# The first normalised rows of a cross attention, prepared two rounds earlier

## The chip, the cores and the metric

The kernel runs on one core of one Trainium2 chip, as one program. Its engines work side by side, each through its own instructions in a fixed order: TensorE (PE) multiplies matrices and transposes, ScalarE (ACT), VectorE (DVE) and GpSimd (POOL) work on elements, and SyncE (SP) issues transfers. Semaphores are the only ties between them. The metric is device time of one execution in microseconds (us), the median of several runs.

## The reference

Four transformer layers follow one another on `x` of 8 batches x 128 rows x 256 numbers, in float32, each attending to the same context. What matters here is where the second ends and the third begins:

```
def _gqa_forward(hidden_state, encoder_hidden_state, ...):      # second layer, 32 heads of 8
    ...
    out = out @ Wo + bo
    x = out + hidden_state
    return (x - mu) * rsqrt(var + EPS) * gamma + beta

def _forward(x, xf_1, xf_2, ...):                               # third layer
    h = _layer_norm(x, ln1_scale, ln1_offset)
    x = res + _cross_attention(h, xf_1, wq1, bq1, wk1, bk1, ...)  # 16 heads of 128
    ...
# in _cross_attention: qh = q_in @ wq + bq ; kh, vh from the context
```

The queries of the third layer need the rows of `x` after the second layer's output, its normalisation and a second one. Keys and values need the context alone.

## The kernel before

`x` lies in on-chip memory (SBUF) as eight batches of 128 rows. The second layer's small heads (`SmallHeads`) run in 16 rounds `r`, two per batch. They are pipelined in an order written out by hand: step `t` of the loop holds the scores of round `t` and later stages of earlier rounds, and steps `R` to `R + 5` (`R` = 16) only empty the pipeline. In step `R + 4` the last batch is transposed (L1167, evacuated by ACT at L1249), multiplied by the output weights (`output(7)`, L1173) and added to `x` by DVE (`add_x(7)`, L1314).

This tail already holds work of the next layer. `n1` is the second layer's normalisation over rows (`statistics` with L1363 and `finish` with L1375, POOL computes the reciprocal deviation at L781 and L783), `first` = `cross.norms[0]` the first normalisation of the third. Batches go in pairs `c`; pairs 0 and 1 are treated in the tail, pairs 2 and 3 later. In steps `R + 2` to `R + 5` PE also projects the cross attention's first four groups of keys (`pe_key`, L1590), which ACT evacuates (`act_key`, L1711).

The third and fourth attention (`CrossLayers`) then start with a part ahead of their loop: PE projects the values of units 0 and 1 (`project_v`, L1618), each followed by the 4 transposes of one pair of normalised rows (`Norm.transposes`, L822); ACT evacuates them with scale and offset into `hT` (L831) and copies them rounded into the high half of `split_sources` (L839); POOL forms the low half, the remainder (`low`, L846). A matmul of this layer is six matmuls, three products of high and low halves for each of two chunks. Then two groups of queries (L1590 again, evacuated by ACT at L1715) need the low halves of batches 0 to 3 (`norm.lo` 4) and the evacuated third and fourth key.

The loop has 128 units of two heads; in step `t` stand the scores of unit `t` (L1632), the transposes of unit `t - 1` (L1643), a projection, the values of unit `t + 2`, the context of unit `t - 2`, the output of unit `t - 3`. DVE takes the maxima (L1808), normalises the probabilities (L1816) and evacuates values (L1803); in its steps 0 to 4 it also handles pairs 2 and 3, beginning with `finish` in step 0. POOL's queue ahead of the loop holds the first value bias (L1882) and small copies of learnt keys (L1904), `low` of pairs 0 and 1, the reciprocal deviations of pairs 2 and 3, `low_wo(0)` (L1897), `low_v(1)` (L1891) and a second value bias.

Of the kernel before, what the change touches and what calls it, by code (L numbers as in the profile page):

```python
# [149 lines left out]
def wait(e, count, value):  # L150

    if isinstance(count, Count):
        e.wait_ge(count.sem, count.base + value)
    else:
        e.wait_ge(count, value)
# [858 lines left out]
class SmallHeads:  # L1014
# [88 lines left out]
    def pe(self, e):  # L1103
        g, l0, project = self.g, self.l0, self.project
# [32 lines left out]
        def context(r):  # L1137
            b, m = self.unit(r)
            if r == 0:
                wait(e, project.vs, 1)  # L1140
            wait(e, self.pt0, r + 1)
            wait(e, self.pt1, r + 1)
            if r >= 1:
                wait(e, self.ot, r)
            PT = self.PT[r % 2]
            for c in range(4):
                mm = e.matmul(self.bC[32 * c:32 * c + 32, :], self.vx[:, b, 4 * m + c, :],
                              PT[:, 512 * c:512 * c + 512], start=True, stop=True)
            mm.then_inc(self.c_full.sem, 1)

        def claim(after):
            if self.last_use:
                wait(e, *self.last_use)
            self.last_use = after
# [35 lines left out]
        for t in range(self.R + 6):  # L1190
            if 0 <= t - 4 < self.R:
                back_transposes(t - 4)
            if t < self.R:
                scores(t)
            if t == 0:
                l0.sum_transposes(e, 6)
                l0.sum_transposes(e, 7)
            if t in (1, 2, 7):
                n = {1: 4, 2: 5, 7: 6}[t]
                claim((project.qk, n + 1))  # L1200
                project.pe_group(e, n)
            if 0 <= t - 2 < self.R:
                transposes(t - 2, 0)
            if self.last_of_batch(t - 5):
                normalised_transposes(self.unit(t - 5)[0])
            if 0 <= t - 3 < self.R:
                context(t - 3)
            if self.last_of_batch(t - 5):
                output(self.unit(t - 5)[0])
            if t == 8:  # L1210
                claim((project.qk, 8))
                project.pe_group(e, 7)
            if t in (9, 11, 13, 15):
                rows_of_first_layer(4 + (t - 9) // 2)
            if 0 <= t - 2 < self.R:
                transposes(t - 2, 1)
            if self.cross and t >= self.R + 2:
                self.cross.pe_key(e, t - self.R - 2)


    def act(self, e):
        g = self.g

        def exps(r, half):
            s = self.sm[r % 3]
            whole = slice(1024 * half, 1024 * half + 1024)
            wait(e, self.shifted, 4 * r + 2 * half + 2)
            a = e.activation(s[:, whole], s[:, whole], ACT.Exp)
            a.then_inc(self.exp.sem, 1)

        def evacuate_t(r, half):
            wait(e, self.t_full, 2 * r + half + 1)
            if r >= 2:
                wait(e, self.c_full, r - 1)
            e.activation(self.PT[r % 2][:, 1024 * half:1024 * half + 1024],
                         self.bT[:, :, :].rearrange("p n t -> p (n t)"), ACT.Copy)\
                .then_inc((self.pt0, self.pt1)[half].sem, 1)

        def evacuate_c(r):
            wait(e, self.c_full, r + 1)  # L1240
            if r >= 2:
                wait(e, self.tb_full, r - 1)
            e.activation(self.oT[r % 2], self.bC[:, :], ACT.Copy).then_inc(self.ot.sem, 1)

        def evacuate_ct(b):
            wait(e, self.ct_full, b + 1)
            if b >= 2:
                wait(e, self.o_full, b - 1)
            e.activation(self.cxT[:, b % 2, :], self.bX[:, 0:D], ACT.Copy).then_inc(self.cx.sem, 1)  # L1249

        for b in range(4, B):
            self.l0.raw(e, b)
        for t in range(self.R + 6):
            if 0 <= t - 2 < self.R:
                exps(t - 2, 1)
            if self.last_of_batch(t - 5):
                evacuate_ct(self.unit(t - 5)[0])
            if 0 <= t - 2 < self.R:
                evacuate_t(t - 2, 0)
            if 0 <= t - 3 < self.R:  # L1260
                evacuate_c(t - 3)
            if t in (1, 2, 7):
                self.project.act_group(e, {1: 4, 2: 5, 7: 6}[t])
            if 0 <= t - 1 < self.R:
                exps(t - 1, 0)
            if t == 8:
                self.project.act_group(e, 7)
            if t in (9, 11, 13, 15):
                self.l0.evacuate_x(e, 4 + (t - 9) // 2)
            if 0 <= t - 2 < self.R:  # L1270
                evacuate_t(t - 2, 1)
            if 3 <= t < 7:
                self.l0.scaled_h(e, t + 1)
            if self.cross and t >= self.R + 2:
                self.cross.act_key(e, t - self.R - 2)


    def dve(self, e):
        g, hd = self.g, self.hd
# [36 lines left out]
        for t in range(self.R + 6):  # L1316
            if 0 <= t - 4 < self.R:
                normalise(t - 4)
            if t < self.R:
                scale_and_mask(t)  # L1320
            if self.last_of_batch(t - 5):
                add_x(self.unit(t - 5)[0])
            if t < self.R:
                maxes(t)
            if t < 2:
                self.l0.stats(e, 4 + 2 * t)
                self.l0.stats(e, 5 + 2 * t)
            if t == 3:
                self.l0.shifts_of_h(e)
            if self.cross:  # L1330
                first = self.cross.norms[0]
                for c in range(2):
                    if t == self.R:
                        self.n1.statistics(e, c)
                    if t == self.R + 1 + c:
                        self.n1.finish(e, c)
                        first.statistics(e, c)
                    if t == self.R + 3 + c:
                        first.normalise(e, c)

    def drained(self):
# [78 lines left out]
class CrossLayers:  # L1420
# [174 lines left out]
    def pe_key(self, e, n):  # L1595
# [3 lines left out]
            wait(e, self.a1.pt1, self.a1.R)  # L1599
        self.project(e, self.first_keys[n])  # L1600

    def pe(self, e):
        g = self.g
        issued = {"t": 0, "v": 0}
# [70 lines left out]
        first = self.norms[0]  # L1675
        for c in range(2):
            project_v(c)
            first.transposes(e, c, g.acc[c])
        for m in self.first_queries:
            self.project(e, m)  # L1680
        for t in range(self.STEPS):
# [63 lines left out]
    def act(self, e):  # L1745
        g = self.g
# [14 lines left out]
                         ACT.Copy).then_inc(self.pt, 1)  # L1761

        first = self.norms[0]
        for c in range(2):
            first.evacuate(e, c, g.acc[c])
        e.wait_ge(self.q_bias, 1)
        self.high_wo(e, 0)
        for m in self.first_queries:
# [1011 lines left out]
```

## Time and profile before

| | before |
|---|---|
| runs, us (median of 3) | 1295.75 (1295.26 to 1298.41) |
| profiled execution, its own time | 1297.17 us |
| its span | 1295.4 us |
| PE busy | 1236.8 us (95%) |
| DVE, ACT, POOL busy | 813.8, 752.7, 569.6 us |
| chain of waits by engine | PE 82%, POOL 6%, DVE 5%, ACT 4% |
| mean granted clock of PE | 0.993 |

A row of the timeline is: start in us from the beginning of the span, duration in us, engine, line of the kernel, operation, what is written and read, count, and in brackets how long the engine had been idle before and what ended that. Several instructions of one kind in a row are merged into one. The chain of waits is followed back from the last instruction: each row has a start, a length and what the time went to; "issue" is time for which the profile shows no cause. A row of the windows has the stretch, its length, busy time with the number of instructions of PE, of PE's weight loads, of DVE, ACT and POOL, then the granted clock of PE as a share of the full one, the share of the transfer engines and GB/s. `l_cols`, `l_w` and the like are names from which a number was left out; `pS`, `pT`, `acc`, `heads_...` are banks of PSUM, where matmuls write.

### The profile page before, as it was taken

The page shows a single profiled execution, that of the slowest core. Times are in us where ns is not written, and L with a number is a line of the kernel's source. Part 1 is how long each engine was busy: PE and PEld are TensorE (multiplying, and loading weights), DVE is VectorE, ACT ScalarE, POOL GpSimd, SP SyncE. Part 2 cuts the span into 40 slices and gives each one's busy share as a digit, 9 for nine tenths or more (in the row PEclk, how much of TensorE's full clock was granted, in tenths as well). Part 3 has the DMA queues.
Part 4 walks back from the last instruction along what each step waited for, and adds up shares of the span by engine and source line. Part 5 has one row for each costly group of instructions (what it writes and reads, how often), then busy time and mean ns, then how long its engine had stood idle before and what let it go on. Part 6 is the DMA issues. An engine that isn't in the chain of part 4 may idle for free.

```text
span 1295.4 us, 24563 instructions
## 1 busy us (share of the span) xinstructions
PE 1236.8 (95%) x8928; PEld 1018.4 (79%) x8928; DVE 813.8 (63%) x1826; ACT 752.7 (58%) x2034; POOL 569.6 (44%) x601
## 2 busy tenths in 40 slices
PE   6999999999988997999999999999999898999899
PEld 5777777777754565899999988999999675878787
DVE  4666666866559785666666776666667514789610
ACT  4765666566557784654555565555554433888842
POOL 3665554556369784150212132322110314899710
PEclk9999999999999998999999999999999999999999
DMA  7101110010100004020202020202000100100000
GB/s 271 52 28 38 43 50 32 28 54 28 59 15 1 1 2 151 13 74 9 74 10 73 10 74 9 74 10 74 10 17 2 68 1 1 66 2 2 2 9 25
DMA packets 15525, 50.44 MB, mean 39 GB/s; under 512 B 1840, under 2 KB 5296, under 8 KB 14384
## 3 DMA queue, kind: packets, MB, share of 16 engines
q1 hardware_dynamic: 15408, 48.87, 11.1%
q8 instruction: 74, 1.21, 0.4%
q14 instruction: 43, 0.35, 0.1%
HBM read 47.82 MB, written 1.05 MB: 38 GB/s over the span
## 4 chain that ended last, share of the span: by engine, by line
PE 82%; POOL 6%; DVE 5%; ACT 4%; issue 2%; DMA 1%; SPq 0%; DVEq 0%; POOLq 0%; ACTq 0%
PE pS L1590 13%; PE pT L1618 7%; PE acc L1670 6%; PE acc L326 6%; PE pT L393 5%; PE pC L406 5%; PE pS L376 4%; PE pS L1632 4%; PE pC L1655 4%; PE acc L362 3%; PE heads_scores L1399 3%; PE heads_scores L1410 3%; POOL probs L2493 2%; PE pT L1643 2%; PE acc L418 2%
## 5 line engine op out<-in xcount | busy, mean ns | idle before, releaser
L1590 PE MATMUL pS<-split_sources,split_pair_weights 128*128 128x512 f32 x768 | 213.1, 413 | 5.8 <-issue 4.3
L717 POOL TENSOR_TENSOR probs<-probs,stats 128x512 f32<-128x512 f32 x128 | 130.5, 1040 | 140.3 <-DVE stats L588 140.3
L523 ACT ACTIVATE probs<-pS,stats 128x256 f32<-128x256 f32 x256 | 117.8, 472 | 99.4 <-DVE stats L583 99.4
L1760 ACT ACTIVATE probsT<-pT 128x256 f32<-128x256 f32 x128 | 49.2, 384 | 197.1 <-PE pT L1643 197.1
L1590 PEld LDWEIGHTS pS<-split_sources,split_pair_weights 128*128 128x128 f32 x768 | 136.5, 191 | 30.9 <-issue 6.6
L1670 PE MATMUL acc<-l_wo_parts,l_ctx_parts 128*128 128x256 f32 x768 | 121.9, 295 | 1.0 <-DVE l_ctx_parts L1832 1.0
L1618 PEld LDWEIGHTS pT<-l_wv_parts,split_sources 128*128 128x128 f32 x756 | 106.9, 188 | 14.2 <-issue 2.2
L1886 POOL TENSOR_TENSOR split_pair_weights<-weights_a,split_pair_weights 128x1024 fp32r<-128x1024 f32 x16 | 38.0, 2381 | 174.1 <-ACT split_pair_weights L1731 174.1
L1618 PE MATMUL pT<-l_wv_parts,split_sources 128*128 128x256 f32 x756 | 110.6, 281 | 2.1 <-issue 2.1
L326 PE MATMUL acc<-split_sources,split_pair_weights 128*128 128x512 f32 x372 | 99.5, 402 | 1.1 <-POOL split_pair_weights L699 0.7
L1670 PEld LDWEIGHTS acc<-l_wo_parts,l_ctx_parts 128*128 128x128 f32 x768 | 99.4, 190 | 1.2 <-DVE l_ctx_parts L1832 1.2
L583 DVE TENSOR_REDUCE stats<-pS 128x2 f32<-128x512 f32 x128 | 82.4, 685 | 28.0 <-PE pS L376 27.8
L1753 ACT ACTIVATE probs<-pS,stats 128x129 f32<-128x129 f32 x256 | 91.3, 366 | 3.5 <-DVE stats L1808 3.3
L1814 DVE RECIPROCAL stats<-stats 128x2 f32<-128x2 f32 x128 | 21.2, 166 | 102.6 <-ACT probs L1753 102.4
L1803 DVE TENSOR_TENSOR v<-pT,probs 128x256 f32<-128x256 f32 x126 | 53.4, 424 | 50.9 <-PE pT L1618 50.8
L1832 DVE SCALAR_TENSOR_TENSOR l_ctx_parts<-pC,l_cols,l_ctx_parts 128x128 fp32r<-128x128 f32 x256 | 78.1, 347 | 4.5
L393 PE MATMUL pT<-consts,probs 128*128 128x128 f32 x512 | 80.5, 280 | 0.1
L1655 PE MATMUL pC<-probsT,v 128*128 128x128 f32 x512 | 77.9, 274 | 1.9 <-DVE l_ctx_parts L1832 1.9
L326 PEld LDWEIGHTS acc<-split_sources,split_pair_weights 128*128 128x128 f32 x372 | 65.5, 189 | 13.0 <-POOL split_pair_weights L699 0.9
L393 PEld LDWEIGHTS pT<-consts,probs 128*128 128x128 f32 x512 | 58.7, 141 | 16.2 <-DVE probsT L592 0.5
L1655 PEld LDWEIGHTS pC<-probsT,v 128*128 128x128 f32 x512 | 67.9, 190 | 2.6 <-ACT probsT L1760 1.7
L376 PEld LDWEIGHTS pS<-l_keys_parts,l_queries_parts 64*128 64x128 f32 x768 | 49.3, 185 | 25.7 <-issue 16.9
(264 smaller groups left out, 2903.5 us busy)
## 6 DMA issues: line engine op xcount, KB each, us to landing
weights_a<-in_l_w SPq DMA_DIRECT2D x16, 768.5 KB, 4.2
weights_a<-in_l_w SPq DMA_DIRECT2D x16, 768.0 KB, 6.0
value_bias_rows<-in_l_bv SPq DMA_DIRECT2D x16, 256.0 KB, 4.5
weights_b<-in_l_wo SPq DMA_DIRECT2D x16, 256.0 KB, 2.6
w_fc<-in_l_w SPq DMA_DIRECT2D x4, 1024.0 KB, 5.8
bias_rows<-in_rows SPq DMA_DIRECT2D x1, 1536.0 KB, 13.5
x_residual<-in_x_dbl SPq DMA_DIRECT2D x2, 512.0 KB, 7.1
masked_scores<-in_ctx_dbl SPq DMA_DIRECT2D x2, 512.0 KB, 8.0
```

The source lines that it names most:

```text
L326: mm = e.matmul(bank[:, :], self.ws[i % 2][kw][:, q, 2 * (m % 2) + c, :], self.zu[c][ks][:, bs, ls], start=j == 0, stop=j == len(PARTS) - 1)
L376: mm = e.matmul(self.S[h][:, it, :], self.q[i % 2][kq][rows, s, it * P:it * P + P], self.k[i % 2][kk][rows, s, :], start=j == 0, stop=j == ...
L393: mm = e.transpose(g.pT[:, (2 * h + it) * P:(2 * h + it + 1) * P], self.E[:, n % 4, h, it, jt * P:jt * P + P], g.ident)
L523: a = e.activation(self.E[:, n % 4, h, it, :], self.S[h][:, it, :], ACT.Exp, bias=self.st[:, 1, n % 4, h, it:it + 1], accum_out=self.st[:, ...
L583: e.tensor_reduce(self.st[:, 1, n % 4, h, :], self.S[h], AX.X, ALU.max, negate=True)\
L717: e.tensor_tensor(self.E[:, n % 4, h, :, :], self.E[:, n % 4, h, :, :], self.st[:, 3, n % 4, h, :].unsqueeze(2).broadcast_to([P, 2, D]), A ...
L1590: mm = e.matmul(bank[:, :], self.w_qk[i % 2][kw][:, 1 - which, c, h * P:h * P + P], g.split[:, which, ks, c, half * HALF:half * HALF + HAL ...
L1618: mm = e.matmul(self.value_bank(n)[:, 0:D], g.split[:, 0, ks, c, b * P:b * P + P], self.w_v[i % 2][kw][:, c, :], start=j == 0, stop=j == l ...
L1655: mm = e.matmul(g.pC[:, h * P:h * P + P], g.v[:, n % B, h * P:h * P + P], self.PT[:, n % 2, h, :], start=True, stop=True)
L1670: mm = e.matmul(g.acc[b // 2][:, (b % 2) * D:(b % 2) * D + D], self.cx[:, n % 2, kc, h, :], self.wo[i % 2][kw][:, h, :], start=first and h ...
L1753: a = e.activation(self.E[:, n % 4, h, :], self.bS[:, h * (P + 1):(h + 1) * (P + 1)], ACT.Exp, bias=self.st[:, 1, n % 4, h:h + 1], accum_o ...
L1832: a = e.scalar_tensor_tensor(out=lo[:, h, :], in0=src[:, h, :], scalar=bias[:, h:h + 1], in1=hi[:, h, :].bitcast(F32), op0=ALU.add, op1=AL ...
```

## The change

The transposes of the pairs 0 and 1 and their evacuation move from the part ahead of the cross attention's loop into step `R + 4` of the heads' loop. On PE they stand behind the transposes of the last batch and ahead of its `output`; on ACT behind the evacuation of the last batch's transposes and ahead of the third and fourth key. DVE normalises pair 1 in step `R + 3`, right behind pair 0, ahead of `add_x(7)`. The banks stay the same; `pe_rows` waits until the heads' last scores have left them. POOL's and SP's orders stay as they are.

```diff
--- before.py
+++ after.py
@@ -1205,6 +1205,9 @@
                 normalised_transposes(self.unit(t - 5)[0])
             if 0 <= t - 3 < self.R:
                 context(t - 3)
+            if self.cross and t == self.R + 4:
+                self.cross.pe_rows(e, 0)
+                self.cross.pe_rows(e, 1)
             if self.last_of_batch(t - 5):
                 output(self.unit(t - 5)[0])
             if t == 8:
@@ -1271,6 +1274,9 @@
                 evacuate_t(t - 2, 1)
             if 3 <= t < 7:
                 self.l0.scaled_h(e, t + 1)
+            if self.cross and t == self.R + 4:
+                for c in range(2):
+                    self.cross.norms[0].evacuate(e, c, g.acc[c])
             if self.cross and t >= self.R + 2:
                 self.cross.act_key(e, t - self.R - 2)
 
@@ -1335,7 +1341,7 @@
                     if t == self.R + 1 + c:
                         self.n1.finish(e, c)
                         first.statistics(e, c)
-                    if t == self.R + 3 + c:
+                    if t == self.R + 3:
                         first.normalise(e, c)
 
     def drained(self):
@@ -1599,6 +1605,10 @@
             wait(e, self.a1.pt1, self.a1.R)
         self.project(e, self.first_keys[n])
 
+    def pe_rows(self, e, c):
+        wait(e, self.a1.scaled, self.a1.R)
+        self.norms[0].transposes(e, c, self.g.acc[c])
+
     def pe(self, e):
         g = self.g
         issued = {"t": 0, "v": 0}
@@ -1675,7 +1685,6 @@
         first = self.norms[0]
         for c in range(2):
             project_v(c)
-            first.transposes(e, c, g.acc[c])
         for m in self.first_queries:
             self.project(e, m)
         for t in range(self.STEPS):
@@ -1761,8 +1770,6 @@
                          ACT.Copy).then_inc(self.pt, 1)
 
         first = self.norms[0]
-        for c in range(2):
-            first.evacuate(e, c, g.acc[c])
         e.wait_ge(self.q_bias, 1)
         self.high_wo(e, 0)
         for m in self.first_queries:
```

PE's order from the heads' last steps to the queries, before (L1167 and L1173 are the last batch's transposes and output, L1590 keys and at the end queries, L1618 values, L822 the transposes of the rows):

```order
L1590 MATMUL pS<-split_sources,split_pair_weights 128x512 x6
L1167 MATMUL heads_output<-consts,v 128x128 x2
L1173 MATMUL heads_output<-w_fc,additive_mask 128x256 x2
L1590 MATMUL pS<-split_sources,split_pair_weights 128x512 x12
L1618 MATMUL acc<-l_wv_parts,split_sources 128x256 x6
L822 MATMUL acc<-consts,normalised 128x128 x4
L1618 MATMUL acc<-l_wv_parts,split_sources 128x256 x6
L822 MATMUL acc<-consts,normalised 128x128 x4
L1590 MATMUL pS<-split_sources,split_pair_weights 128x512 x12
```

and in the changed kernel, where L1596 is the projection and L1628 the values:

```order
L1596 MATMUL pS<-split_sources,split_pair_weights 128x512 x6
L1167 MATMUL heads_output<-consts,v 128x128 x2
L822 MATMUL acc<-consts,normalised 128x128 x8
L1173 MATMUL heads_output<-w_fc,additive_mask 128x256 x2
L1596 MATMUL pS<-split_sources,split_pair_weights 128x512 x12
L1628 MATMUL acc<-l_wv_parts,split_sources 128x256 x12
L1596 MATMUL pS<-split_sources,split_pair_weights 128x512 x12
```

The 8 transposes left the places behind each group of values and stand ahead of the output. Keys, values and queries follow one another.

ACT's order at the same place, before (L1711 key evacuations, L1249 the last batch, L831 and L839 the rows, L1715 queries):

```order
L1711 ACTIVATE kT<-pS,l_cols 128x4x128 x2
L1249 ACTIVATE additive_mask<-heads_output 128x256
L1711 ACTIVATE probs<-pS,l_cols 128x4x128 x2
L831 ACTIVATE hT<-acc,bias_cols 128x128 x4
L839 ACTIVATE split_sources<-hT 128x2x128 x2
L831 ACTIVATE hT<-acc,bias_cols 128x128 x4
L839 ACTIVATE split_sources<-hT 128x2x128 x2
L1743 ACTIVATE l_wo_parts<-weights_b 128x512
L1715 ACTIVATE qT<-pS,l_scaled_query_bias 128x512 x2
```

and in the changed kernel (L1720, L1252 and L1724 are the same three lines, L1752 is L1743):

```order
L1720 ACTIVATE kT<-pS,l_cols 128x4x128 x2
L1252 ACTIVATE additive_mask<-heads_output 128x256
L831 ACTIVATE hT<-acc,bias_cols 128x128 x4
L839 ACTIVATE split_sources<-hT 128x2x128 x2
L831 ACTIVATE hT<-acc,bias_cols 128x128 x4
L839 ACTIVATE split_sources<-hT 128x2x128 x2
L1720 ACTIVATE probs<-pS,l_cols 128x4x128 x2
L1752 ACTIVATE l_wo_parts<-weights_b 128x512
L1724 ACTIVATE qT<-pS,l_scaled_query_bias 128x512 x2
```

The last two keys' evacuations stand behind the rows instead of ahead of them.

DVE, from the heads' last `normalise` (L1305) on, before:

```order
L1305 TENSOR_TENSOR v<-heads_output,stats 128x128
L815 TENSOR_SCALAR normalised<-x_residual,stats 128x256 x2
L1314 TENSOR_TENSOR x_residual<-heads_output,x_residual 128x256
L815 TENSOR_SCALAR normalised<-x_residual,stats 128x256 x2
L1803 TENSOR_TENSOR v<-acc,probs 128x256 x2
L771 BN_STATS stats<-x_residual 128x6 x2
```

and in the changed kernel (L1311, L1320 and L1810 are the same lines as L1305, L1314 and L1803):

```order
L1311 TENSOR_TENSOR v<-heads_output,stats 128x128
L815 TENSOR_SCALAR normalised<-x_residual,stats 128x256 x4
L1320 TENSOR_TENSOR x_residual<-heads_output,x_residual 128x256
L1810 TENSOR_TENSOR v<-acc,probs 128x256 x2
L771 BN_STATS stats<-x_residual 128x6 x2
```

Pair 1 moved ahead of the last addition to `x`.

## Rows read from the trace of the kernel before

**Rows 1.** Windows: stretch, its us, then busy time and clock by engine.

```profile
484.00:492.00 8.00, 6.24 (x50) 3.76 (x49) 6.27 (x23) 5.61 (x8) 4.12 (x7) 1.00 0.01 3
...
497.00:503.50 6.50, 6.22 (x36) 5.34 (x36) 1.82 (x5) 2.71 (x7) 0.47 (x4) 1.00 0.51 184
...
503.50:507.79 4.29, 0.00 (x1) 0.03 (x1) 4.29 (x12) 3.52 (x11) 3.02 (x5) 0.91 1.02 375
...
507.79:510.50 2.71, 2.71 (x7) 2.13 (x8) 0.58 (x2) 0.00 (x0) 2.46 (x5) 0.50 0.87 328
```

**Rows 2.** Chain of waits, the end of the heads to the first scores.

```profile
497.28 1.13 PE heads_output L1173 x4
...
498.41 2.80 PE pS L1590 x12
...
501.20 0.71 PE acc L1618 x6
...
501.92 0.44 PE acc L822 x4
...
503.50 4.29 issue
...
507.79 5.47 PE pS L1590 x12
...
514.03 0.71 PE pS L1632 x4
```

**Rows 3.** Timeline, the heads' last step, four engines.

```profile
495.54 0.73 DVE L815 TENSOR_SCALAR normalised<-x_residual,stats 128x256 f32<-128x256 f32 x2
...
495.55 0.76 POOL L783 TENSOR_TENSOR stats<-stats,eps 128x2 f32<-128x2 f32 x1
...
496.06 0.38 PE L1167 MATMUL heads_output<-consts,v 128*128 128x128 f32 x2
...
496.23 0.72 POOL L1882 TENSOR_TENSOR probs<-value_bias_rows 128x256 f32<-128x256 f32 x1
...
496.85 0.38 ACT L1249 ACTIVATE additive_mask<-heads_output 128x256 f32<-128x256 f32 x1
```

**Rows 4.** Timeline, ACT and POOL while the normalised rows are prepared.

```profile
501.24 0.69 ACT L1711 ACTIVATE probs<-pS,l_cols 128x512 f32<-128x512 f32 x1 [0.72 <-PE pS L1590]
...
502.39 1.50 ACT L831 ACTIVATE hT<-acc,bias_cols 128x128 f32<-128x128 f32 x4 [0.46 <-PE acc L822]
...
504.28 1.60 POOL L846 TENSOR_TENSOR split_sources<-hT,split_sources 128x256 fp32r<-128x256 f32 x2 [6.81 <-ACT split_sources L839]
...
505.75 0.75 ACT L839 ACTIVATE split_sources<-hT 128x256 fp32r<-128x256 f32 x2
...
506.28 1.41 POOL L846 TENSOR_TENSOR split_sources<-hT,split_sources 128x256 fp32r<-128x256 f32 x2 [0.40 <-ACT split_sources L839]
```

**Rows 5.** Timeline, DVE: statistics without and beside POOL's subtractions.

```profile
484.30 0.74 DVE L771 BATCH_NORM_STATS2 stats<-x_residual 128x6 f32<-128x256 f32 x2
...
485.96 0.75 DVE L771 BATCH_NORM_STATS2 stats<-x_residual 128x6 f32<-128x256 f32 x2
...
504.39 1.77 DVE L1363 SCALAR_TENSOR_TENSOR x_residual<-x_residual,stats,bias_rows 128x256 f32<-128x256 f32 x2
```

**Rows 6.** Timeline, POOL, DVE and PE around the loop's first step.

```profile
510.04 1.28 POOL L1897 TENSOR_TENSOR l_wo_parts<-weights_b,l_wo_parts 128x512 fp32r<-128x512 f32 x1
...
511.27 1.30 POOL L1891 TENSOR_TENSOR l_wv_parts<-weights_a,l_wv_parts 128x512 fp32r<-128x512 f32 x1
...
515.12 0.87 DVE L1375 SCALAR_TENSOR_TENSOR x_residual<-x_residual,stats,bias_rows 128x256 f32<-128x256 f32 x2
...
517.54 0.41 PE L1643 MATMUL pT<-consts,probs 128*128 128x128 f32 x2 [0.23 <-DVE v L1803]
```

**Rows 7.** Timeline, DVE beside POOL in a later step of the loop.

```profile
758.66 2.38 POOL L1886 TENSOR_TENSOR split_pair_weights<-weights_a,split_pair_weights 128x1024 fp32r<-128x1024 f32 x1
...
759.79 1.54 DVE L1816 TENSOR_TENSOR probs<-probs,stats 128x256 f32<-128x256 f32 x1
```

## The prediction

> **What bounds the kernel now.** I read the page's share of the engines first: TensorE (PE) is busy for 95% of the span and holds 82% of the chain of waits, so time is won only where PE waits, or where its clock is low. The clock row of the page has one dip near the middle. The windows around it [rows 1] show what it is: PE works without a break until 503.50, has nothing to do for 4.29 us, and then runs at a granted clock of 0.50 (1.2 of 2.4 GHz). From 484 to 492, where it was busy for 6.24 of 8 us in shorter pieces, the clock stayed at 1.00. The chain of waits names the same place [rows 2]: the last output of the heads, two keys, the values, then "issue 4.29", and two query projections that take 5.47 us for 12 matmuls, where two key projections of the same shape took 2.80.
>
> What PE waits for at 503.50 stands in the code: a query projection needs `norm.lo` 4, the low halves of the first four batches of normalised rows. The timeline of ACT and POOL gives the order [rows 4]. The transposes of the rows stand behind the last output, two keys and a value; only then can ACT evacuate and round them (502.39 to 506.50), and POOL's last subtraction ends at 507.69, 0.10 before PE goes on. Yet DVE has the first pair of rows at 496.27 [rows 3]. PE waits for a chain ACT, POOL that starts 5 us later than its data allow.
>
> **The change part by part.** No instruction is added or removed: PE still issues 8 transposes, ACT 8 scale-and-shift evacuations and 4 copies, DVE 4 normalisations. All move.
>
> 1. *DVE.* The second pair is normalised directly behind the first, ahead of the last `add_x`. It needs its reciprocal deviation from POOL, ready at 495.55 + 0.76 = 496.31, when DVE is free. Unhindered the pair would take 0.73, to 497.1. But POOL starts the value bias at 496.23, for 0.72 [rows 3]. Below I show DVE and POOL keeping each other out; so the pair starts at 496.95 and ends at 497.6.
>
> 2. *PE.* The first 4 transposes fall into PE's wait for ACT (from 496.06 + 0.38 to 497.28 [rows 2, 3]) and cost nothing. The second 4 (0.44 [rows 2], then between the value groups) start at about 497.1 to 497.6, so that the last output starts at 497.6 to 498.1 instead of 497.28. I take 498.1, by the POOL row: 0.8 lost. `add_x(7)` and the loads that wait for it come as much later, which nothing near waits for.
>
> 3. *ACT.* It is free at 497.23 [rows 3]. Evacuations and copies took 505.75 + 0.75 - 502.39 = 4.11 [rows 4], so they now end at 501.3. The second pair is in its bank long before ACT comes to it. Behind them are now queued the third and fourth key evacuation, 0.69 each [rows 4], done at 502.0 and 502.7; the fourth was done at 501.9 before. PE needs the third for the first query, the fourth for the second.
>
> 4. *POOL.* Its last subtraction ended 1.19 after ACT's last copy (507.69 and 506.50); now at 502.5.
>
> 5. *PE again.* From its start at 498.1 the output takes 1.13, the keys 2.80, two value groups 0.71 each [rows 2]: the queries can start at 503.45. Rows (502.5) and third key (502.0) are there, with 0.9 to spare, so the wait of 4.29 is gone. PE has then no idle stretch before the queries, so they run as the keys do, 2.80, and end at 506.25. From the end of the queries to the first scores it was 514.03 - 513.26 = 0.77, ACT's evacuation; so scores at 507.0 instead of 514.0. As a sum: 4.29 (wait) + 2.67 (clock) + 0.88 (transposes out of the path) - 0.8 (late output) = **7.0 us**.
>
> 6. *What is late next.* DVE must be done with two value evacuations and the statistics of the other four batches. These started 503.52; without POOL beside them one pair takes 485.96 - 484.30 = 1.66 [rows 5]. Now values end at 504.0, statistics at 507.3. `finish` began 1.09 after the scores (515.12 and 514.03 [rows 2, 6]), with the first maxima just ahead of it; so DVE is wanted at about 507.7 and in time by 0.4. But POOL is not as far as before. Its chain follows DVE's statistics: last aggregate at about 506.6, a microsecond of reciprocal deviations (its longer instruction took 0.76 [rows 3]), then `low_wo` 1.28, `low_v` 1.30 and a value bias of 0.72, from 507.7 to 511. Before they lay from 510.04 on [rows 6], in DVE's idle time ahead of the first scores at 514.03; now they fall on the first step of the loop, on `finish` (two instructions, 0.87), then `normalise`. PE's first transposes stand behind all three.
>
> What that costs has rows of its own. A `normalise` of the loop took 1.54 us and ended at 761.33, 0.29 after the POOL subtraction that ran since 758.66 [rows 7]. Two scalings of `statistics` took 1.77 beside two POOL subtractions that took 1.60 [rows 4, 5], where the two of `finish`, of the same form, took 0.87 [rows 6]. Strictly, with the engines taking turns: `finish` asks at 508.1, gets in at 509.0, its second half at 510.7, `normalise` at 511.9. The first transposes, 3.51 after the scores before (517.54 - 514.03 [rows 2, 6]), or 510.5, would start at 512.6: 2.1 lost. At 0.45 each, as in rows 5 and 6 ((1.77 - 0.87) / 2), it is 1.35; with luck nothing. I take 2.0, since POOL's pieces here are long as in rows 7. PE works in order and has no idle time there to make it up. Net: 7.0 - 2.0 = **5.0 us**.
>
> The Trainium skill, SBUF — State Buffer, "SBUF: two separate sides", says that VectorE and GpSimd share a port pair as an exclusive lock: an instruction with two SBUF inputs, or a VectorE one in a two-port mode, waits for the whole of the other's. The two ends in rows 7 agree; it speaks for the 2.1 over the 1.35. By it the gain is 4.9, by 0.45 each 5.65.
>
> After the first steps every wait is relative to the loop's own beat, weights are loaded many steps ahead, and PE is the bound; a shift is kept to the end.
>
> The profiled execution took 1297.17 us, 1.42 more than the median of the runs, 1295.75. It would take 1292.2; the runs' median I put at 1295.75 - 5.0 = **1290.8**.
>
> **The rivals.**
> - *A, no collision.* POOL and DVE miss each other or the overlap is cheap; the output is only 0.3 late. Gain 7.0 + 0.5 - 0 = 7.5: 1288.3, down to 1289.7 with half of it. For it: POOL's pieces follow the end of DVE's statistics, and if these end half a microsecond earlier `low_wo` is over before `finish` asks. Against: `low_v` then takes its place, and rows 7.
> - *B, the clock falls anyway.* The tail of the heads is thin in PE work, and could bring the low level later, at the queries: 2.67 comes back and more of the first step. Gain 5.0 - 2.67 = 2.3 or less: 1293.4. Against: it stayed at 1.00 through 484 to 492 in the same tail.
> - *C, slower.* The low clock comes and lasts into the loop. A step holds 6 wide matmuls (1.4 at full clock, 2.7 at half), 6 of half their width and transposes, some 2 us more per step. With the queries' 2.67 gone too, 2.3 is left, so from the second slow step on the kernel is slower than before; three give 1299.5. Against: in rows 1 it came only behind 4.29 us of nothing.
> - *D, the wait moves.* The change doesn't do what it says: the second pair of rows, behind POOL's bias and its small copies, holds the output back by 2 to 3 us instead of 0.8, and keys, values and scores with it. PE then has the old idle time in another place. Gain 2.5 to 3.5: 1292.3 to 1293.3. Against: POOL's copies are 128x8.
>
> **How the numbers follow.** Forecast 0.53 (1289.7 to 1291.9), A 0.22, B 0.08, C 0.04, D 0.13. The range from A's end to B's and D's is 1288.0 to 1293.2, and leaves out C and the outer parts, under 0.2. A measurement here can tell about 0.3%, 3.9 us, from no change: the line is 1291.9. Below it lie A and nearly all of the forecast, 0.74; between are B, D and the forecast's edge, 0.22; slower 0.04.
>
> **What would show it.** In the profile after: 8 transposes at 496.4 to 498.1, ahead of the last output; no idle stretch of PE over 1 us from there to the scores; granted clock 1.00 throughout 497 to 520; the 12 query matmuls in about 2.8; first scores near 507; DVE's `finish` drawn out beyond 1.5 us beside `low_wo` and `low_v`, and PE waiting for DVE about 2 us before the first transposes of the loop. Steps from the third on should repeat before, shifted by 5. Wrong would be: a query that still waits for POOL, a low clock, or first scores later than 509; and, for the size, `finish` at 0.87 would make it 7.

## The result and the profile after

The changed kernel takes 1293.55 us (median of 12 runs, 1290.98 to 1294.46); the kernel before took 1296.84 in the runs made beside them (12 runs, 1295.02 to 1300.62). The ratio is 0.9969, with a 95% interval of 0.9961 to 0.9977: faster by 4.0 us (3.0 to 5.1). The two medians lie only 3.3 us apart, because the 12 runs of before hold the three that were known ahead of the forecast; the nine others have a median of 1297.62, to which the ratio fits. Forecast were a gain of 5.0 and a time of 1290.8 within 1288.0 to 1293.2. The time itself lies 0.35 us above that range. The kernel before also lay higher this time than the 1295.75 from which the forecast started, and 1295.75 times the ratio is 1291.7; so the gain is the number to compare.

The windows of the changed kernel (columns as in [rows 1]):

```profile
484.00:492.00 8.00, 6.24 (x52) 4.03 (x50) 6.30 (x23) 6.10 (x8) 4.63 (x8) 1.00 0.01 3
497.00:503.50 6.50, 5.95 (x35) 5.10 (x36) 1.64 (x4) 6.38 (x17) 4.03 (x9) 1.00 0.32 101
503.50:508.00 4.50, 3.72 (x20) 2.83 (x20) 3.92 (x14) 1.52 (x3) 2.12 (x4) 1.00 1.00 420
508.00:512.00 4.00, 2.69 (x18) 2.22 (x16) 3.80 (x5) 1.50 (x5) 3.83 (x4) 1.00 0.96 338
```

Where before had 4.29 us without PE work and then half the clock, PE is busy for 3.72 of 4.50 us and the clock stays at 1.00. What is new is the last row: PE busy for 2.69 of 4.00 us.

The chain of waits over the same place, beside [rows 2]:

```profile
496.86 1.11 DVE normalised L815 x2
...
498.11 0.63 PE acc L822 x4
498.74 0.87 PE heads_output L1173 x4
499.61 2.79 PE pS L1596 x12
502.40 1.43 PE acc L1628 x12
503.83 2.82 PE pS L1596 x12
...
507.41 0.73 PE pS L1642 x4
...
508.51 2.75 DVE x_residual L1381 x2
...
512.60 0.41 PE pT L1653 x2
```

The queries follow the values without a gap and take 2.82 us for 12 matmuls, and scores begin at 507.41 instead of 514.03. This profile runs half a microsecond late from the start (the heads' last maxima begin at 478.94; before, at 478.41), so the gain up to the scores is 6.62 + 0.53 = 7.15. Then the chain goes through DVE for 2.75 us, and PE's first transposes stand at 512.60, 5.19 behind the scores, where it had been 3.51 [rows 2, 6]. Gain there: 517.54 - 512.60 + 0.53 = 5.47.

Why DVE is late is in the timeline of DVE and POOL:

```profile
496.06 1.90 DVE L815 TENSOR_SCALAR normalised<-x_residual,stats 128x256 f32<-128x256 f32 x4
...
496.75 0.73 POOL L1889 TENSOR_TENSOR probs<-value_bias_rows 128x256 f32<-128x256 f32 x1
...
498.58 1.03 PE L1173 MATMUL heads_output<-w_fc,additive_mask 128*128 128x256 f32 x4
...
508.24 1.29 POOL L1904 TENSOR_TENSOR l_wo_parts<-weights_b,l_wo_parts 128x512 fp32r<-128x512 f32 x1
508.51 2.75 DVE L1381 SCALAR_TENSOR_TENSOR x_residual<-x_residual,stats,bias_rows 128x256 f32<-128x256 f32 x2
...
509.49 1.48 POOL L1898 TENSOR_TENSOR l_wv_parts<-weights_a,l_wv_parts 128x512 fp32r<-128x512 f32 x1
...
510.93 0.90 POOL L1889 TENSOR_TENSOR probs<-value_bias_rows 128x256 f32<-128x256 f32 x1
...
511.36 0.76 DVE L1823 TENSOR_TENSOR probs<-probs,stats 128x256 f32<-128x256 f32 x1
...
512.04 0.41 DVE L1810 TENSOR_TENSOR v<-pT,probs 128x256 f32<-128x256 f32 x1
```

`finish` (L1381; 0.87 in [rows 6]) takes 2.75. It starts 0.27 us after `low_wo` has begun, and the two engines take turns: POOL's `low_v` needs 1.48 instead of 1.30, its value bias 0.90 instead of 0.72, DVE's normalisation (L1823) 0.76 instead of 0.43. Behind it stands one more evacuation of values (L1810), which PE's transposes wait for. At the top the four row normalisations (L815) take 1.90 beside the first value bias, where two pairs took 0.73 each before.

From step 1 of the loop to the last layer the two profiles run in parallel: DVE's maxima in the loop, from the second of the 128 on, are 4.84 to 4.98 us earlier, nearly all of them 4.87. Near 1077, in the last layer, the distance drops from 5.03 to 3.34. The row of the changed kernel, and its windows there:

```profile
1077.60 5.38 PE L1416 MATMUL heads_scores<-w_fc,hidden_b 128*128 128x256 f32 x16 [1.53 <-DVE masked_scores L2431]
```

```profile
1076.00:1078.00 2.00, 0.47 (x6) 0.41 (x3) 1.77 (x2) 0.00 (x0) 0.38 (x1) 1.00 0.00 0
1078.00:1080.00 2.00, 2.00 (x7) 1.59 (x6) 0.58 (x1) 0.00 (x0) 2.00 (x2) 0.51 0.04 8
1080.00:1082.00 2.00, 2.00 (x8) 1.62 (x7) 0.00 (x0) 0.00 (x0) 2.00 (x3) 0.63 0.00 0
```

The same 16 matmuls in the profile of the kernel before:

```profile
1082.63 3.69 PE L1410 MATMUL heads_scores<-w_fc,hidden_b 128*128 128x256 f32 x16 [1.53 <-DVE masked_scores L2424]
```

5.38 instead of 3.69: 1.69 us, lost to a granted clock of 0.50 that the profile of before doesn't have there. Not one instruction of the last layer was changed. The last layer has a second such place, between 1210 and 1240. On balance both profiles lose 1.7 us there (before has low stretches at 1220 and 1231, the changed kernel one at 1228), so the distance is 3.35 ahead of it and 3.41 behind. The spans are 3.4 us apart (1295.4 and 1292.0).

### The profile page after: what moved, and what is told of

It reads as the page before. It is cut to its first block, busy times and chain, and to the rows that moved or that the text cites. A ratio compares the mean times of both kernels' runs of the same rounds, so it can differ in the third digit from the quotient of the medians.

```text
span 1292.0 us, 24565 instructions
## 1 busy us (share of the span) xinstructions
PE 1234.9 (96%) x8928; PEld 1016.8 (79%) x8928; DVE 814.9 (63%) x1826; ACT 753.3 (58%) x2034; POOL 570.3 (44%) x601
## 4 chain that ended last, share of the span: by engine, by line
PE 81%; POOL 6%; DVE 6%; ACT 5%; issue 2%; DMA 1%; SPq 0%; DVEq 0%; ACTq 0%; POOLq 0%
PE pS L1596 13%; PE pT L1628 7%; PE acc L1680 6%; PE acc L326 6%; PE pT L393 5%; PE pC L406 5%; PE pS L376 4%; PE pS L1642 4%; PE pC L1665 4%; PE acc L362 3%; PE heads_scores L1405 3%; PE heads_scores L1416 3%; POOL probs L2500 2%; PE pT L1653 2%; PE acc L418 2%
## 5 line engine op out<-in xcount | busy, mean ns | idle before, releaser
L1596 PE MATMUL pS<-split_sources,split_pair_weights 128*128 128x512 f32 x768 | 210.5, 409 | 1.5 <-POOL split_sources L846 1.5
L1596 PEld LDWEIGHTS pS<-split_sources,split_pair_weights 128*128 128x128 f32 x768 | 134.8, 188 | 25.9 <-issue 2.1
L1628 PEld LDWEIGHTS pT<-l_wv_parts,split_sources 128*128 128x128 f32 x756 | 106.9, 188 | 14.2 <-issue 2.2
L1628 PE MATMUL pT<-l_wv_parts,split_sources 128*128 128x256 f32 x756 | 110.6, 281 | 2.1 <-issue 2.1
L1810 DVE TENSOR_TENSOR v<-pT,probs 128x256 f32<-128x256 f32 x126 | 53.4, 424 | 50.4 <-PE pT L1628 50.4
```

What stands on the lines that cost most here:

```text
L1596: mm = e.matmul(bank[:, :], self.w_qk[i % 2][kw][:, 1 - which, c, h * P:h * P + P], g.split[:, which, ks, c, half * HALF:half * HALF + HAL ...
L1628: mm = e.matmul(self.value_bank(n)[:, 0:D], g.split[:, 0, ks, c, b * P:b * P + P], self.w_v[i % 2][kw][:, c, :], start=j == 0, stop=j == l ...
```

## The experiments

Ratios are to runs of before on the same chip. "Scores" is the start of the loop's first scores on PE, counted from the start of the heads' last maxima on DVE (before: 514.03 - 478.41 = 35.62; changed: 507.41 - 478.94 = 28.47), which takes out what comes earlier. "Step" is the distance from the first scores to the loop's first transposes (before 3.51, changed 5.19), and the last column is the granted clock at the first place in the last layer, between 1075 and 1095 us, with the length of the low stretch.

| kernel | median us | ratio (95%) | scores | step | 1075 to 1095 |
|---|---|---|---|---|---|
| changed, again | 1293.42 | 0.9968 (0.9954 to 0.9981) | 28.47 | 5.20 | low, 3.4 us |
| before, filled | 1295.96 | 0.9986 (0.9977 to 0.9996) | 33.20 | 3.50 | low, 3.4 us |
| POOL's order | 1288.66 | 0.9931 (0.9917 to 0.9946) | 28.49 | 3.51 | full |
| one pair | 1296.72 | 0.9990 (0.9981 to 1.0000) | 33.64 | 3.49 | low, 6.8 us |
| before, again | 1299.32 | 1.0012 (0.9999 to 1.0026) | 35.50 | 3.52 | low, 3.4 us |
| bias early | 1291.12 | 0.9953 (0.9937 to 0.9969) | 28.10 | 5.18 | full |
| all three | 1290.40 | 0.9947 (0.9932 to 0.9963) | 28.24 | 3.51 | low, 3.4 us |
| all three, filled | 1292.53 | 0.9964 (0.9951 to 0.9976) | 28.20 | 3.51 | low, 3.4 us |
| POOL's order, again | 1290.55 | 0.9946 (0.9927 to 0.9965) | 28.48 | 3.49 | low, 3.4 us |
| order and bias | 1289.16 | 0.9939 (0.9921 to 0.9957) | 28.10 | 3.50 | full |

**The changed kernel again.** No edit.

> The changed kernel again, unaltered. Its profile of before the study lost 1.69 us in the last layer, where 16 matmuls took 5.38 instead of 3.69 at a granted clock of 0.50 for 3.4 us. Theory 'chance of phase': that low stretch hangs on when the thin piece of PE work falls, not on the change; another execution may show it, or not (then the profile ends 1.7 us earlier, or the low stretch lies elsewhere). Rival 'caused by the change': the low clock stands at the same place (about 1077 to 1082) again. Time against before by both: ratio 0.996 to 0.998.

1293.42 us, ratio 0.9968. The profile agrees to a few hundredths: scores 28.47, queries 2.82, `finish` 2.75, step 5.20, and again a low stretch near 1077, for 1.58 us this time (the 16 matmuls take 5.27). Alone this favours "caused by the change"; the later runs show kernels of every kind with it.

**The kernel before, its idle stretch filled.**

```diff
             first.transposes(e, c, g.acc[c])
+        wait(e, self.a1.ot, self.a1.R)
+        for j in range(18):
+            c, kw, ks = PARTS[j % 6]
+            e.matmul(g.pT[:, :], self.w_qk[0][kw][:, 1, c, 0:P], g.split[:, 0, ks, c, 0:HALF],
+                     start=j % 6 == 0, stop=j % 6 == 5)
```

> The kernel before, with 18 more matmuls 128x512 of the shape of the key projections (4.2 us of PE work at full clock, results unused) in PE's idle stretch of 4.29 us ahead of the queries. Theory 'the clock is a term of its own, 2.67 us': the queries still start near 507.8 but their 12 matmuls take 2.8 instead of 5.47, first scores near 511.4 instead of 514.0, and then part of it is lost as DVE meets POOL in the first step (0 to 1); time 1.7 to 2.7 us below before. Rival 'the low clock has another cause than PE's rest (the transfers of that stretch, or its place)': the queries take 5.5 again and the time is that of before.

The chain of waits of this kernel:

```profile
503.37 4.20 PE pT L1682 x18
...
507.72 3.05 PE pS L1590 x12
...
511.52 0.73 PE pS L1632 x4
```

and its windows over the fill and the queries:

```profile
503.40:507.60 4.20, 4.17 (x18) 3.01 (x16) 4.20 (x12) 3.50 (x11) 3.07 (x4) 1.00 0.93 366
507.70:510.80 3.10, 3.03 (x12) 2.16 (x12) 0.59 (x2) 0.71 (x2) 2.85 (x5) 1.00 0.73 292
```

The queries start where they did (507.72) and take 3.05 instead of 5.47, at a granted clock of 1.00. So rest on PE, not POOL's late rows, cost this part, and 18 useless matmuls save 2.4 us on the path. The transfers of that stretch ran on at 366 GB/s (375 before) without bringing the clock down, which rules them out. The time fell by 1.8 us (0.5 to 3.0); this profile had the low stretch near 1080 and lost 1.3 there.

**One pair.** As the changed kernel, but pair 1 normalised, transposed (behind both groups of values) and evacuated where it had been.

```diff
                 self.cross.pe_rows(e, 0)
-                self.cross.pe_rows(e, 1)
...
-                    if t == self.R + 3:
+                    if t == self.R + 3 + c:
...
             project_v(c)
+        first.transposes(e, 1, g.acc[1])
...
         first = self.norms[0]
+        first.evacuate(e, 1, g.acc[1])
```

> The change made for the first pair of batches alone: the second pair is normalised, transposed (behind the values) and evacuated where it was. PE should be idle for about 3.3 us ahead of the queries (rows at 502.7, ACT 2.0, POOL 1.2). Theory 'wait and clock are two terms': the wait gives 1 us back; if the clock stays at 1.00 over a rest of 3.3 us, another 2.67 comes on top and first scores lie near 510.2; if it falls as before, near 513. Rival 'what counts is the order of the output and the keys, not the rows': time as the changed kernel, 3 to 4 us below before.

```profile
500.00:502.50 2.50, 2.46 (x19) 2.13 (x17) 0.80 (x3) 0.69 (x2) 0.01 (x1) 1.00 0.92 383
502.50:506.15 3.65, 0.00 (x0) 0.03 (x1) 3.65 (x13) 2.63 (x7) 1.68 (x3) 0.99 0.98 411
506.15:510.70 4.55, 4.54 (x12) 3.31 (x12) 0.18 (x1) 0.69 (x1) 4.30 (x6) 0.63 0.74 260
```

PE waits for 3.65 us instead of 4.29, and the clock falls here too: over the queries it is 0.63, and they take 4.56. The first scores come 2.0 us earlier than before (33.64 against 35.62), at 511.48, between my two numbers. The rival (order of output and keys) is wrong: 5.2 of the 7.15 us hang on the second pair. In the time little of it is left (ratio 0.9990); in this profile, of the slowest of its 12 executions, the clock was low for 6.8 us near 1080, and for 6.8 again near 1230.

**POOL's order ahead of the loop.**

```diff
-        n1.rstd_of(e, 2)
-        n1.rstd_of(e, 3)
-        self.low_wo(e, 0)
         self.low_v(e, 1)
+        self.low_wo(e, 0)
+        n1.rstd_of(e, 2)
+        n1.rstd_of(e, 3)
         self.value_bias(e, 1)
```

> The changed kernel, with POOL's low halves of the second pair's value weights and of the first output weights put ahead of the two reciprocal deviations instead of behind them; value bias stays last. Theory 'the drawn-out first step (finish 2.75, PE waits 1.91 for its first transposes) is DVE and POOL keeping each other out': finish falls to about 0.9 to 1.3, PE's first transposes of the loop come 3.5 after the first scores (near 511) instead of 5.2 after them, 1.3 to 1.7 us gained over the changed kernel; statistics may lose 0.3. Rival 'DVE is late for another reason (it simply has too much in that step)': finish stays above 2 us or the transposes stay 5.2 behind the scores, and the time is that of the changed kernel.

Timeline of POOL, DVE and PE in this kernel:

```profile
502.72 1.31 POOL L1898 TENSOR_TENSOR l_wv_parts<-weights_a,l_wv_parts 128x512 fp32r<-128x512 f32 x1
...
503.98 1.30 POOL L1904 TENSOR_TENSOR l_wo_parts<-weights_b,l_wo_parts 128x512 fp32r<-128x512 f32 x1
...
504.99 0.96 DVE L1369 SCALAR_TENSOR_TENSOR x_residual<-x_residual,stats,bias_rows 128x256 f32<-128x256 f32 x2
...
508.34 0.87 DVE L1381 SCALAR_TENSOR_TENSOR x_residual<-x_residual,stats,bias_rows 128x256 f32<-128x256 f32 x2
...
509.50 0.43 DVE L1823 TENSOR_TENSOR probs<-probs,stats 128x256 f32<-128x256 f32 x1
...
510.59 0.73 POOL L1889 TENSOR_TENSOR probs<-value_bias_rows 128x256 f32<-128x256 f32 x1 [2.40 <-DMA value_bias_rows<-in_l_bv]
...
510.76 0.41 PE L1653 MATMUL pT<-consts,probs 128*128 128x128 f32 x2 [0.23 <-DVE v L1810]
```

`low_v` and `low_wo` now run beside value evacuations and the statistics' first instructions. Those read PSUM or a single SBUF operand, and only one scaling pays 0.1. `finish` is back at 0.87, the normalisation at 0.43, the step at 3.51: the collision was the whole of the 1.68 us. The value bias could not have gone forward as well; it waited 2.4 us for its rows from memory. But the time fell by 4.8 us against the changed kernel, three times what I expected.

**Where the rest came from.** The same kernel again:

> The kernel with POOL's order changed once more: is its 1288.7 to be had again? Theory 'it gained 1.65 in the first step and was spared the 1.65 of low clock in the last layer by chance': time between 1288.5 and 1291, and where the profile shows a low stretch near 1075 to 1085, that execution is 1.7 longer. Rival 'the order itself is worth 4.5 to 5': 1288.7 again with full clock in the last layer.

1290.55, in runs from 1288.59 to 1291.90, where the first group had 1288.25 to 1289.90. Through the loop the two profiles lie 0.3 us apart, but their spans are 1286.9 and 1289.9. The 3 us are lost in the last layer, at two places. The first, in the first profile and in the second:

```profile
1075.78 3.69 PE L1416 MATMUL heads_scores<-w_fc,hidden_b 128*128 128x256 f32 x16 [1.53 <-DVE masked_scores L2431]
```

```profile
1075.50 5.38 PE L1416 MATMUL heads_scores<-w_fc,hidden_b 128*128 128x256 f32 x16 [1.54 <-DVE masked_scores L2431]
```

3.69 and 5.38 in one and the same kernel. The second place, again in the first and in the second:

```profile
1223.97 1.09 PE L2173 MATMUL heads_transposed<-consts,masked_scores 128*128 128x128 f32 x8 [1.07 <-ACT masked_scores L2311]
1224.90 1.89 PE L1405 MATMUL heads_scores<-hT,w_fc 128*128 128x256 f32 x8
```

```profile
1225.32 1.53 PE L2173 MATMUL heads_transposed<-consts,masked_scores 128*128 128x128 f32 x8 [2.44 <-ACT masked_scores L2311]
1226.64 3.17 PE L1405 MATMUL heads_scores<-hT,w_fc 128*128 128x256 f32 x8
```

The second profile loses another 1.7 us here. The first had its low stretch at 1213 already, and the 1.4 us lost there came back in a shorter wait (1.07 instead of 2.44). So the first profile with POOL's order gained about 1.7 us three times over the changed kernel: by the collision, and at both places of the last layer. That accounts for the 4.8; only the first of the three is shown to be the order's own.

And the kernel before:

> The kernel before once more, for its clock in the last layer. Of six profiles so far, before and the one with POOL reordered show full clock behind the thin piece of PE work near 1080, four others (the changed kernel twice, the filled one, the one with one pair) show 0.50 for 3.4 to 6.8 us. Theory 'chance of the execution': before may show it as well, and its low stretches near 1210 to 1230 may number one or two. Rival 'it belongs to kernels whose last layer begins earlier': before shows full clock there again. Time as before, ratio 1.000.

```profile
1082.19 3.69 PE L1410 MATMUL heads_scores<-w_fc,hidden_b 128*128 128x256 f32 x16 [1.53 <-DVE masked_scores L2424]
...
1089.09 5.38 PE L1410 MATMUL heads_scores<-w_fc,hidden_b 128*128 128x256 f32 x16 [1.43 <-DVE probs L2424]
```

In this execution it keeps its clock at the place where the changed kernel lost it, and loses it one round later; it takes 5.38 there, where the first profile of before took 3.69. Between 1200 and 1240 its clock stays at 1.00, where the first profile of before was low twice. So the low stretch doesn't need the change. Between 1075 and 1095 it comes in 8 of 12 profiles, in kernels of every kind, and can be there and missing in the same kernel; between 1210 and 1240 it comes in 11.

Whether it is equally likely in every kernel is another matter. The mean granted clock of every run is on record: it was 0.995 or 0.996 in all 19 runs of the changed kernel, and 0.997 in 8 of the 11 with POOL's order. In the profiles of these two kernels 0.996 goes with two low stretches in the last layer and 0.997 with one. So no run of the changed kernel seems to have been spared at both places, though its last layer holds the same instructions. What decides is open: around 1080 PE does the same work in all of them, but for the one with a fill, and is idle for 1.1 to 1.2, then 1.5, 0.6 and 1.4 us between small pieces.

**Bias early.** The first value bias and the learnt keys' copies ahead of the tail's last reciprocal deviation.

```diff
-            for c in range(2):
-                self.cross.norms[0].rstd_of(e, c)
+            self.cross.norms[0].rstd_of(e, 0)
+            wait(e, self.t_full, 2 * self.R)
+            self.cross.value_bias(e, 0)
+            self.cross.learnt_keys(e, 0)
+            self.cross.learnt_keys(e, 1)
+            self.cross.norms[0].rstd_of(e, 1)
...
-        wait(e, self.a1.t_full, 2 * self.a1.R)
-        self.value_bias(e, 0)
-        self.learnt_keys(e, 0)
-        self.learnt_keys(e, 1)
```

> The changed kernel, with POOL's first value bias and its four small copies put ahead of the last reciprocal deviation of the heads' tail instead of behind it. Theory 'the second pair's normalisation (1.11 on the path) is held by the value bias that POOL starts 0.1 earlier': the four normalisations take about 1.45 instead of 1.90, and output, keys and first scores come 0.3 to 0.5 earlier against the changed kernel. Rival 'the delay is DVE's wait for the deviation itself': no change. In time 0.3 to 0.5 us, too little for the clocks of these runs; the profile decides.

```profile
495.32 1.54 DVE L815 TENSOR_SCALAR normalised<-x_residual,stats 128x256 f32<-128x256 f32 x4
...
497.01 0.63 PE L822 MATMUL acc<-consts,normalised 128*128 128x128 f32 x4 [0.18 <-DVE normalised L815]
```

The four normalisations take 1.54 instead of 1.90, and the second transposes wait 0.18 for DVE instead of 0.55: 0.37 gained, as expected, and the same at the scores (28.10 against 28.47). Up to the loop that is all. But the wait of 1.9 us in the first step, which the changed kernel passed at full clock, was followed here by a low stretch:

```profile
508.00:512.00 4.00, 2.08 (x15) 1.81 (x14) 3.96 (x8) 1.08 (x4) 2.71 (x3) 1.00 0.75 293
512.00:516.00 4.00, 4.00 (x19) 3.59 (x18) 1.64 (x7) 1.70 (x6) 0.93 (x2) 0.60 0.69 240
```

**All three** (order, early bias, and the second pair's transposes behind the output; only this third part is shown).

```diff
                 self.cross.pe_rows(e, 0)
-                self.cross.pe_rows(e, 1)
...
                 output(self.unit(t - 5)[0])
+            if self.cross and t == self.R + 4:
+                self.cross.pe_rows(e, 1)
```

> The changed kernel with POOL's order in the loop's head changed (as measured: 1288.7), value bias early, and the second pair's transposes behind the last output instead of ahead of it. The latter takes 0.44 from ahead of the output to behind it, which only helps add_x; with the bias early the output no longer waits for DVE, so the first scores should come 0.8 to 1.0 us earlier than in the changed kernel (its 0.8 of late output gone), at about 13.3 us behind the start of the heads' last step output. Expected 1287.7 to 1288.4. Rival 'DVE or POOL binds now': the first scores come earlier and the first transposes do not, time 1288.7.

1290.40, above the 1287.7 to 1288.4 expected. Scores 28.24, step 3.51, and a low stretch at either place of the last layer. The chain of this kernel at the output:

```profile
497.00 1.13 PE heads_output L1177 x4
498.13 0.44 PE acc L822 x4
498.57 2.80 PE pS L1601 x12
```

The output starts at 497.00, 18.87 behind the heads' last maxima, as in the kernel before (497.28 - 478.41): its lateness of 0.8 is gone. But the 0.44 of transposes lies on the path behind it now, which I had overlooked; 0.24 is left at the scores instead of 0.8 to 1.0. Keeping the order and the early bias alone is better (28.10).

**All three, filled in the last layer.**

```diff
+        wait(e, m2.gelu, 8)
+        for j in range(2):
+            e.matmul(self.bT[:, 0, :], self.wk[1][:, j % 2, 0:P], g.cT[:, j % 2, 0:HALF], start=True, stop=True)
         for t in range(self.STEPS):
...
                 scores(t)
+            if t == 0:
+                wait(e, m2.gelu, 8)
+                for j in range(3):
+                    e.matmul(self.bT[:, 0, :], self.wk[1][:, j % 2, 0:P], g.cT[:, j % 2, 0:HALF],
+                             start=True, stop=True)
```

> All three, and in the last layer two and three more matmuls 128x512 (0.43 each, results unused) in PE's idle pieces of 1.1 and 1.5 us around the first scores. Theory 'the low clock there comes from the thin work around 1075': the granted clock is 1.00 from 1060 to 1100, and against all_three the time is 1.7 less in executions that had the low stretch, or 0 to 0.3 more if all_three has none. Rival 'it comes from elsewhere (POOL and DVE work, or a rhythm of its own)': a low stretch may stand there in spite of the fill.

```profile
1077.13 3.62 PE L1421 MATMUL heads_scores<-w_fc,hidden_b 128*128 128x256 f32 x16
...
1083.96 5.35 PE L1421 MATMUL heads_scores<-w_fc,hidden_b 128*128 128x256 f32 x16 [1.43 <-DVE probs L2440]
```

The filled place keeps its clock, and the low stretch comes one round later (5.35 there), against the expectation. That the fill moved it isn't shown: the kernel before, run again, had it one round later without any fill, and four profiles without a fill have full clock at both rounds. The fill is also too long: DVE's maxima behind it are 1.4 us nearer to those of before than ahead of it. The median, 1292.53, lies 2.1 us above that of all three without the fill.

**Order and bias.** POOL's order and the early bias, transposes as in the changed kernel.

> POOL's order changed and the first value bias early, the second pair's transposes ahead of the output as in the changed kernel. First scores 0.3 to 0.4 earlier than with the order alone, first transposes 3.5 behind them; 0.3 us in time if the clock does the same in both, else up to 1.7 either way.

1289.16, ratio 0.9939. Scores 0.39 earlier than with the order alone (28.10 and 28.49), step 3.50, full clock near 1080 and a low stretch at 1225. It and the kernel with POOL's order (1288.66 and 1290.55) can't be told apart; both are faster than the changed kernel (1293.4 to 1293.6), by the 1.7 us that the profiles show in the loop's first step and by what the clock does in the last layer.

## Why the prediction was right, and where its sum was off

*The wait and the clock.* Both terms came as worked out: the wait of 4.29 is gone, the queries take 2.82 (2.80 forecast). The filled kernel shows that they are two terms, since with the clock alone 2.4 us come back.

*The late output.* Forecast was 0.8 by POOL's value bias holding back the second pair, start 498.1; measured 498.58, or 498.05 without this profile's 0.53. The early bias gave 0.37 of it back; the rest, 0.4, is what the second pair's transposes take on PE, since with the early bias and the transposes behind the output none of the 0.8 is left there (all three). The first scores were to be 7.0 us earlier and are 7.15.

*DVE against POOL.* This was the step that spoke against the change, and it happened at its place: `finish` and the normalisation drawn out, transposes late by 5.19 - 3.51 = 1.68, where the strict working gave 2.1 and the sum took 2.0. The turns began where I had placed them (`finish` starts at 508.51 - 0.53 = 507.98, forecast 508.1). Two errors of size then partly cancelled. The turns were shorter: DVE's instruction ended 0.28 to 0.29 behind POOL's in each (`finish` at 511.26 behind `low_v` at 510.97, the normalisation at 512.12 behind the value bias at 511.83), where I had let it begin only then and take its whole 0.43; so the normalisation was done at 511.6 on the forecast's scale instead of 512.3. And the forecast left out the value evacuation (0.42) between it and the transposes; with it the strict working would have given 2.3. The Trainium skill (SBUF — State Buffer, "SBUF: two separate sides") has the shared pair as an exclusive lock; the trace agrees, as `low_v` and the value bias are lengthened in their turn by 0.18 each. So the two engines hold each other up here without any semaphore between them. The kernel with POOL's order makes it shown, not argued: with the same instructions in another order all of the 1.68 is gone.

*What the sum lacked.* "A shift is kept to the end" was the step that failed: the sum put the clock of the last layer at nothing. The distance of 4.87 us (5.40 with the late start counted) held to 1075 us, and then 1.69 went to a low clock near 1077, where the first profile of before had none. At the second place, between 1210 and 1240, both lost 1.7. What is left, 3.41, or 3.94 with the late start, is the measured 4.0; that the 5.0 missed by only 1.0 is partly because the loop gained 0.4 more than forecast. Why the low clock came is open. The change isn't needed for it, since the kernel before shows it too; but the granted clock of its 19 runs never reached the 0.997 of the kernels with POOL's order, so luck alone isn't shown either. I named a low clock as rival B, but at the queries, where it didn't come.

*The rivals.* A (no collision) is refuted by `finish` at 2.75; the kernel with POOL's order then does what A describes, by an edit and not by luck. B and C didn't happen in the changed kernel; the early bias shows C's beginning once, 0.60 over 512 to 516. D is wrong in its size, since the output lost 0.8 and not 2 to 3.

## What to carry to other kernels

When a late chain is moved forward, look at what its lateness had been hiding: POOL's pieces had run in the pause that the change removed, and met DVE once it was gone. Price a PE pause of 4 us at its length and at half the clock behind it. And before a microsecond of gain is believed or missed, look for low clock in thin stretches elsewhere, in more than one profile: here each is worth up to 1.7 us, and two profiles of one kernel ended 3.0 us apart by them.

## What the runs showed of the hardware

- Eighteen matmuls whose results nobody reads, put into a pause of 4.29 us, made a kernel faster (ratio 0.9986, 0.9977 to 0.9996): the granted clock over the queries behind it was 1.00 instead of 0.50.
- A rest of 3.65 us was followed by the low level (0.63 over the next 4.55 us), one of 1.91 us in the loop's first step sometimes: not in the changed kernel's two profiles, but with the bias early (0.60 over 4 us).
- Around 1080 us PE is idle for at most 1.5 us at a time, and yet the clock fell to 0.50 in 8 of 12 profiles, for 3.4 us in seven and 6.8 in one, at one of two rounds. Between 1210 and 1240 it fell in 11 of 12. One kernel can show it in one execution and not in the next.
- One low stretch cost nothing lasting: the one at 1213 (POOL's order) drew PE's work out by 1.4 us, and PE's next wait for ACT was 1.07 instead of 2.44.
- DVE and POOL in turns lengthen each other: an operation of 0.43 took up to 1.54 [rows 7], and two of POOL's three took 0.18 more each. Value evacuations out of PSUM ran beside `low_v` and `low_wo` at their usual 0.42.
